# 16-head attention on one core: value products of two steps put behind one another, twelve probability tiles instead of eight

## The reference, cut to what matters

```python
B, S, D, H, Dh = 8, 512, 256, 16, 16          # ctx: (8, 1601, 256)
v = (ctx @ Wv.T).reshape(B, -1, H, Dh)
k = (ctx @ Wk.T).reshape(B, -1, H, Dh)
q = (layernorm(x) @ Wq.T).reshape(B, -1, H, Dh)
energy = einsum('nqhd,nkhd->nhqk', q, k)
attn = softmax(energy / sqrt(256), axis=3)
out = einsum('nhql,nlhd->nqhd', attn, v).reshape(B, -1, H * Dh)
x = x + tanh(g_xattn[0]) * (out @ Wo.T + bo)
```

## Time and profile before

| | |
|---|---|
| median of 3 runs | 3453.11 us (3452.84 to 3453.65) |
| the profiled execution's own time | 3450.29 us |
| its span, first to last instruction | 3448.6 us |
| mean granted TensorE clock | 0.969 of full speed |
| first and last score matmul of the stage start at | 285.5 and 1409.0 us |
| busy shares of the whole program | PE 96%, DVE 72%, ACT 46%, POOL 13% |

### The profile page before, as it was taken

How to read it: one execution, slowest core, us unless ns; L and a number is a source line. 1 busy time by engine, 2 the same in 40 slices (tenths; PEclk the granted TensorE clock), 3 DMA queues, 4 the chain that set the end, 5 groups by cost and what they waited for, 6 DMA issues and landing times. The chain is left out here.

```text
span 3448.6 us, 61045 instructions
## 1 busy us (share of the span) xinstructions
PE 3297.8 (96%) x21500; PEld 1953.3 (57%) x21500; DVE 2483.1 (72%) x5513; ACT 1602.0 (46%) x2882; POOL 452.9 (13%) x538
## 2 busy tenths in 40 slices
PE   9988999999999999769979999969999999999999
PEld 5652222222222222458854444549888898888988
DVE  5557889898989897340026565478888888888885
ACT  5534888888888888312214344322222222222221
POOL 0022111111111110120014242300000000000000
PEclk9987999999999999879989999979999999999999
DMA  7687666576757560232111221130000000000000
GB/s 279 244 237 92 99 103 104 100 107 97 109 95 108 86 89 22 98 116 94 36 56 65 79 83 63 44 131 12 12 9 11 12 11 12 9 11 12 11 12 7
DMA packets 148231, 256.70 MB, mean 74 GB/s; under 512 B 23848, under 2 KB 99472, under 8 KB 147536
## 3 DMA queue, kind: packets, MB, share of 16 engines
q1 hardware_dynamic: 132752, 218.29, 29.9%
q0 software_dynamic: 10288, 31.21, 2.7%
q10 hardware_dynamic: 5008, 5.00, 0.5%
HBM read 170.38 MB, written 83.64 MB: 74 GB/s over the span
## 5 line engine op out<-in xcount | busy, mean ns | idle before, releaser
L725 DVE TENSOR_REDUCE at_pmax<-at_psm 128x2 f32<-128x1024 f32 (+1 forms) x832 | 945.0, 1179 | 133.1 <-PE at_psm L553 128.3
L662 ACT ACTIVATE ring<-at_pss 128x512 f32<-128x512 f32 (+1 forms) x1664 | 895.2, 595 | 204.3 <-PE at_pss L577 201.0
L577 PE MATMUL at_pss<-at_qs,at_ks 99*128 99x512 bf16 (+1 forms) x1664 | 514.2, 388 | 14.0 <-ACT ring L662 7.2
L1836 PE MATMUL mt_psd<-mt_xl,mt_key_in 128*128 128x128 f32 x4096 | 491.8, 279 | 0.1
L1836 PEld LDWEIGHTS mt_psd<-mt_xl,mt_key_in 128*128 128x128 f32 x4096 | 470.4, 193 | 1.6 <-DMA mt_key_out<-m_out 0.3
L1862 PE MATMUL mt_psu<-mt_key_out,mt_g 128*128 128x256 f32 x2048 | 447.4, 379 | 1.3 <-DVE mt_g L2073 1.3
L585 PE MATMUL at_pso<-ring,at_vw 128*32 128x512 f32 (+1 forms) x3328 | 445.9, 608 | 0.0
L1862 PEld LDWEIGHTS mt_psu<-mt_key_out,mt_g 128*128 128x128 f32 x2048 | 386.7, 190 | 52.6 <-DVE mt_g L2073 1.4
L577 PEld LDWEIGHTS at_pss<-at_qs,at_ks 99*128 99x128 bf16 (+1 forms) x1664 | 116.3, 98 | 491.8 <-ACT ring L662 429.9
L1924 ACT ACTIVATE mt_g<-mt_psd 128x512 f32<-128x512 f32 x256 | 152.8, 597 | 349.9 <-PE mt_psd L1836 349.6
L551 PE MATMUL at_psm<-at_ks,at_qs 64*128 64x512 bf16 (+1 forms) x1024 | 273.0, 345 | 11.7 <-DVE at_pmax L725 9.3
(11 more groups left out here) (232 smaller groups left out, 4199.5 us busy)
## 6 DMA issues: line engine op xcount, KB each, us to landing
at_ks<-k_dram SPq DMA_DIRECT2D x192, 200.1 KB, 6.5
k_dram<-pj_kp SPq DMA_DIRECT2D x24, 800.5 KB, 5.2
xs_dram<-at_qf POOLq DMA_DIRECT2D x68, 256.0 KB, 3.2
v_dram<-pj_v SPq DMA_DIRECT2D x8, 1664.0 KB, 6.6
at_vd<-v_dram SPq DMA_DIRECT2D x32, 416.0 KB, 10.5
wide_ctxT<-ctxT SPq DMA_DIRECT2D x8, 1601.0 KB, 7.3
at_kh<-k_dram SPq DMA_DIRECT2D x124, 100.1 KB, 5.4
at_qs<-q_dram SPq DMA_DIRECT2D x192, 64.0 KB, 6.7
```

The lines of the kernel that those rows point to most:

```text
L577: nc.tensor.matmul(ps_s[0:r, score_slot(u, n), :], ks[:, g, j, kt * P:kt * P + r], qs[:, g, j, :], start=True, stop=True).then_inc(s_mm, 1)
L662: nc.scalar.activation(pr[0:r, (NST * g + n) % PRING, :], ps_s[0:r, score_slot(u, n), :], ACT.Exp, scale=SCALE).then_inc(expd, 1)
L725: nc.vector.tensor_reduce(heads, found, AX.X, ALU.max).then_inc(m_red, 1)
L1836: ins = nc.tensor.matmul(ps_d[:, j % 2, y * P:y * P + P], key_in[:, k, j * YB + y, :], xl[:, s, k, :], start=k == 0, stop=k == KC - 1)
```

## The change

The ring of probabilities has twelve tiles: the eight of `ring`, and four new ones in a buffer `more`. The combined weight matrices, which had buffers of their own, now lie in `more` before the first tile is written there; the zeros that clear a DRAM buffer have their own buffer `zero`. The value products are issued in even steps only, for the blocks of both steps (eight products), and step 13 issues its own four. The waits for the widened values and for the copied sums stand in step 2 instead of step 1. The number of instructions of each kind is the same.

```diff
--- before.py
+++ after.py
@@ -350,7 +350,8 @@
 
 
     SLOTS = G
-    PRING, SBANKS, MBANKS = 8, 3, 2
+    PRING, SBANKS, MBANKS = 12, 3, 2
+    MORE, TOGETHER = PRING - 8, 2
     NST = KT * HG
     MSPAN = 512
     NFULL, REST = KEYS // MSPAN, KEYS % MSPAN
@@ -387,8 +388,15 @@
         kh, qh = st.sb("kh", [P, SLOTS, HG // 2, KEYS], BF16), st.sb("qh", [P, SLOTS, HG // 2, S], BF16)
         vd = st.sb("vd", [P, 2, KT * HG, DH])
         vw = st.sb("vw", [P, 2, KT * HG, 2 * DH])
-        pr = t["ring"]
-        full = {n: st.sb(n + "f", [P, KC, D]) for n in "qkv"}
+        more = st.sb("more", [P, MORE, S])
+
+        def prob(n):
+
+            n %= PRING
+            return t["ring"][:, n, :] if n < PRING - MORE else more[:, n - (PRING - MORE), :]
+
+        full = {n: more[:, i, :].rearrange("p (k d) -> p k d", d=D) for i, n in enumerate("qkv")}
+        zero = st.sb("zero", [P, KC, D])
         pmax, nmax = st.sb("pmax", [P, HG, QT, NM]), st.sb("nmax", [P, HG * QT])
         mfull, mrest, mpart = st.sb("mfull", [HG * QT, P]), st.sb("mrest", [HG * QT, P]), st.sb("mpart", [HG * QT, 3, P], BF16)
         acc, den, o = (t["quad"][:, i, :] for i in (0, 2, 3))
@@ -583,7 +591,7 @@
 
                     pe.wait_ge(expd, u * NST + n + 1 + SBANKS)
                     nc.tensor.matmul(ps_o[j * 32:(j + 1) * 32, :], vw[0:r, g % 2, kt * HG + j, :],
-                                     pr[0:r, (NST * g + n) % PRING, :], start=kt == 0, stop=kt == KT - 1).then_inc(pv, 1)
+                                     prob(NST * u + n)[0:r], start=kt == 0, stop=kt == KT - 1).then_inc(pv, 1)
 
                 def first_scores(u, g):
 
@@ -618,12 +626,13 @@
                                 scores(u + 1, nxt[1], j)
                             if kt == TURN_AT and j == 0 and nxt is not None:
                                 turn_max(u + 1)
-                        if kt == 1:
+                        if kt == TOGETHER:
                             pe.wait_ge(v_wide, u + 1)
 
                             pe.wait_ge(acc_out, u + 1)
-                        for j in range(HG):
-                            values(u, g, (kt - 1) * HG + j)
+                        if kt % TOGETHER == 0 or kt == KT:
+                            for n in range((kt - 1) // TOGETHER * TOGETHER * HG, kt * HG):
+                                values(u, g, n)
 
                 last = B - 1
                 for n in range(NJ):
@@ -659,7 +668,7 @@
 
                         act.wait_ge(pv, u * NST + n + 1)
                         act.wait_ge(s_mm, u * NST + n + 1)
-                        nc.scalar.activation(pr[0:r, (NST * g + n) % PRING, :], ps_s[0:r, score_slot(u, n), :],
+                        nc.scalar.activation(prob(NST * u + n)[0:r], ps_s[0:r, score_slot(u, n), :],
                                              ACT.Exp, scale=SCALE).then_inc(expd, 1)
                         if n == TURN_BEHIND and u + 1 < UNITS:
                             turned_out(u + 1)
@@ -802,7 +811,7 @@
                 def clear(n):
 
                     for block_ in blocks[n * PER_UNIT:(n + 1) * PER_UNIT]:
-                        pool.dma_start(block_.rearrange("(k p) d -> p k d", p=P), full["q"][:, :, :]).then_inc(t["zeroed"], 16)
+                        pool.dma_start(block_.rearrange("(k p) d -> p k d", p=P), zero[:, :, :]).then_inc(t["zeroed"], 16)
 
                 spread(0, 0, False)
                 spread(0, 1, False)
@@ -810,7 +819,7 @@
                 add_bias()
                 split(1)
                 pool.wait_ge(mixed_out, 5)
-                nc.gpsimd.memset(full["q"][:, :, :], 0.0).then_inc(biased, 1)
+                nc.gpsimd.memset(zero[:, :, :], 0.0).then_inc(biased, 1)
                 pool.wait_ge(biased, 2 + NT // QT)
                 for i in range(1, UNITS // 2):
                     for s in range(2):
```

## The result

The changed kernel takes 3581.24 us (median of 4 runs, 3577.94 to 3582.53), the kernel before 3453.11 us. The ratio is 1.037, with a 95% interval of 1.0358 to 1.0382: 128 us slower, where 134 were forecast. The profiled execution took 3582.23 us.

The account below looks back on a forecast made before the run. PE was taken as nearly full, DVE at 89% with only two PSUM pairs. Units growing from 34.8 to 39.3 us give 130, with ends 130 - 2 + 4 + 2 = +134: 3587 us, range 3566 to 3612.

Parts of the forecast that it names:

- The saving on PE: PE over two steps: one change from scores to values and one back removed, 5.05 instead of 5.22 us, 0.17 less.
- The wait for DVE: Fourth job of a pair waits for its banks, 2.84 us after the first; with 3.29 more, a pair takes 6.13.
- The wait for ACT: Fifth and sixth score tiles of a pair wait for exponentials; without any other wait the pair would take 5.50 us.
- DVE's pieces at nothing: DVE's other pieces, before jobs 14, 16 and 18, cost nothing; if all exposed, 0.8 us a unit, 24 in all.
- Steps 9 and 10: In this pair the short jobs lift the DVE wait, but the transpose waits for an exponential: about 6.0 us.
- A unit: Thirteen steps: 5 x 6.13 + 6.0 + 2.61 = 39.3 us against 34.8; 29 intervals give +130.
- The ends: Outside the intervals: unit 0 costs 0, the clock after its idle -2, unit 30 +4, the last unit +2 us.
- The shares: Busy shares in the stage after the change: near 82% for PE and 79% for DVE.
- A: Rival: neither wait binds, a pair costs 5.05 us and the kernel is 33 us faster, 3420; chance 3%.
- B: Rival: the DVE wait is hidden and only ACT's remains, 5.50 us a pair, +25, kernel 3478; chance 6%.
- D: Rival: more than the two waits; clock falls for one pair in ten, 3663, or DVE's pieces exposed, 3611; chance 9%.
- C: Rival: nothing to be measured, within 0.2% or 7 us; gain and waits cancel, 5.22 to 5.35 a pair; chance 2%.

Follow-up runs that it names:

- short reductions: Each reduction over 256 of its 512 keys, other half left out: changed kernel 3492.69 us, kernel before 3430.18 us.
- short exponentials: Changed kernel with exponentials of 256 of 512 queries only, that half read twice by the value products: 3570.89 us.
- five banks: Changed kernel with five score banks instead of three, each job making one head's products, read twice: 3640.31 us; same edit on the kernel before: 3441.77 us.
- the ring alone: Changed kernel's twelve probability tiles and moved buffers, but value products in every step as in the kernel before: 3453.32 us, ratio 0.9998.
- uneven jobs: Kernel before with both jobs of maxima before the first score tile in even steps, before the last in odd ones: 3613.58 us, ratio 1.0466.
- jobs spread again: Changed kernel with the eight value products between the jobs in even steps, except pairs 9 to 10: 3637.17 us, ratio 1.0538.
- the run without waits: Changed kernel with five score banks, one head's products per job, and reductions over half the keys: 3413.68 us; kernel before with the same edits: 3415.97 us.

## Why the prediction was right, point by point

*The saving on PE.* Forecast 0.17 us for a pair. Measured in the changed kernel a little more: eight value products to the next score took 1.86 where I took 1.90, and without waits the pair is 5.02 for 5.05. I had chosen the upper of two readings of a pass (0.42 to 0.45); the lower was nearer. The saving is real and shows only when both waits are gone (0.20).

*The wait for DVE.* The step that decides the result, and it held to the hundredth: 2.84 from the first job to the fourth, 6.11 for a pair against 6.13. Shown by three runs: shorter reductions take it away, moved jobs make it without any grouping, more score banks leave it as it is.

*The wait for ACT.* The prediction lists 5.05, 5.50 and 6.13 one after another, but its 6.13 is DVE's circle alone (2.84 + 3.29) and holds no term of ACT's. That is how it came out. Alone, ACT's wait is real (5.48 with short reductions, 5.50 forecast). Beside DVE's it costs a pair nothing, as the run with short exponentials and the one with five banks show.

*DVE's pieces at nothing.* Right within 0.1 us: they fall into DVE's idle time, which is 1.49 us in a pair without them. The prediction gave that time as 1.1; its own terms make it 1.4 (6.13 + 0.97 less 5.7). Of the 0.87 us before, the short reductions take away 0.75 (34.05 us for a unit), so that much is waits for DVE. Cutting the pieces takes away 0.29; how much more of it they cause is not shown.

*Steps 9 and 10.* Mis-sized: 6.0 forecast, 5.86 in the runs. I let the transpose wait for an exponential; the row beside the transposes above puts its wait down to the last reduction of maxima (DVE L739, 37.4 us in all, matmuls and weight loads together).

*A unit.* 39.3 forecast, 39.06 measured. 29 intervals give +123 instead of +130.

*The ends.* They were forecast at +4 in all. The two profiled spans differ by 131.9 us, so outside the intervals it is +8.6: 3.3 before unit 1 begins, 2.7 from there to its transpose, 2.6 behind the last transpose. The total came nearer than its parts: the units were 7 us too high and the ends 4.6 too low, and the medians lie 3.8 us closer together than the profiled runs. That much of the agreement is luck.

Unit 0 was to cost nothing, because PE waits for POOL there. PE did begin unit 1 3.28 us later (333.04 for 329.76). POOL's additions to x in the changed kernel:

```profile
309.61 18.56 POOL L803 TENSOR_TENSOR x_rows<-x_rows,at_bo 128x1024 f32<-128x1024 f32 x8
```

In the trace of before they began at 306.31, 3.30 us earlier, with the same length. The order of the value products is not the cause, since the run of the ring alone has them at 310.18. The six experiments on the kernel before, without any part of the change, have them between 307.19 and 309.30, later than its own trace by up to 3.0 us. So most of the 3.3 us lies within what the traces differ by anyway; what moves the start is not shown. The clock after this wait fell to 0.50 as before, though PE had stood for 4.48 us instead of 6.59: my -2 for it was not there in the profiled run. In the run with uneven jobs PE stood for 2.26 us at this place, and the mean of the same window (329.70 to 339.20) was 0.64.

*The shares.* 79% for DVE came out, 82% for PE did not: it is 90%. The 82% is 5.05 in 6.13, from start to start. The profile's matmuls have modelled ends that cover part of a wait: of the 0.46 and 0.61 us lost before the sixth score tile and the fourth job, the rows show 0.18 and 0.45 as idle, and 0.63 of 6.11 is 10%.

*The rivals.* A (no wait binds) is out, and so is B (only ACT's wait); B is just what the short reductions produce. D named a fall of the clock. The changed kernel kept 1.00, but two experiments on it (five score banks, jobs spread again) did not, so the chance given to D was no luxury. C's 5.22 to 5.35 was wider than its 7 us: 0.13 us for a pair is 25 us.

## What to carry to other kernels

When two engines hand work over through two buffers, what counts is the distance between hand-overs on the producer, not only the work of each: here 2.30 us of reductions fitted a step of 2.61 as long as two jobs came every 2.61. They cost 0.9 us a pair of steps when PE's own work put the same jobs 1.5 and then 3.5 us apart (580.70, 582.20 and a pair of 5.02 in the run without waits). Before work is grouped to save changes of kind, write down the circle (job starts, consumer done, buffer free, job again) for the longest and the shortest distance; the saving counts only if both still fit. And waits that lie beside one another aren't a sum: taking the smaller away gave nothing.

## What the runs showed of the hardware that was not expected

The granted clock did not follow the sum of PE's idle time. From 400 to 1500 us, mean granted clock and PE's busy time in three kernels with the same matmuls:

| | PE busy of 1100 us | clock |
|---|---|---|
| changed kernel | 993.95 | 1.00 |
| uneven jobs | 962.60 | 1.00 |
| jobs spread again | 977.02 | 0.96 |

The one with the most idle time kept its clock, and one with less did not (the busy time of the last is in part at the lower clock).

Five score banks gave 0.93 and 41.66 us for a unit, though a pair at full clock is 6.09 there. That kernel took 59 us more than the changed one, although the same edit made the kernel before 11 us faster. A wait that lies in one piece doesn't explain it: the short exponentials have nearly the same pair (third job to fourth 1.05 us, where it is 1.13 with five banks; 6.11 for 6.09) and kept 1.00. What else sets the five banks apart is that half the products of maxima are left out (5014 matmuls in the window for 6237). That alone doesn't lower the clock, since the kernel before with five banks has them left out too and keeps 1.00 (400 to 1340 us). Whether the two together do it was not tried, and the spread jobs fell to 0.96 with all products in place. The cause stays open.
